# A graph network on one core: the six products of a split adjacency tile in another order, with both waits ahead of them

## The chip, the cores and the metric

The kernel runs on one core of one Trainium2 chip. The metric is the device time in microseconds (us) of one execution. The kernel before took 1182.28 us, the median of 3 runs (1181.62 to 1182.28).

## The reference

Four graph layers run one after the other over the same 4096 x 4096 adjacency matrix `adj` and a 4096 x 128 feature matrix `x`, each followed by a residual sum and a layer norm:

```python
deg = clip(sum(adj, axis=1), 1.0)
x = layernorm(x + x @ L0_W_self + (adj @ x / deg) @ L0_W_neigh)
x = layernorm(x + relu(adj @ (x @ L1_kernel) + L1_bias))
h = relu(adj @ (x @ L2_W1) + b1);  h = relu(adj @ (h @ L2_W2) + b2)
x = layernorm(x + h)
n1 = swish((adj @ x) @ L3_W + b);  n2 = swish((adj @ n1) @ L3_W + b)
x = layernorm(x + n2)
```

So the adjacency matrix is multiplied six times by a 4096 x 128 operand. Everything is float32.

## The kernel before

Six passes (numbered 0 to 5) go over the adjacency matrix, one for each product with it. A pass makes 8 chunks of 512 output columns, and a chunk is summed in one bank of `agg` over 16 tiles of 128 x 1024 (two blocks of 512 columns, which are two steps of the contraction). Of a chunk's tiles 14 come again in each pass from HBM into the 7 slots of `ring`, and two stay in `kept` from pass 0 on.

For speed the float32 product is taken apart. ScalarE casts a tile to the rounded type, `adj_hi` (`hi_tile`, L417). VectorE subtracts it from the tile and leaves the rest in `adj_lo` (`lo_tile`, L538). The operand has such halves too, `op_hi` and `op_lo`. A tile then costs TensorE six products of 128 x 512: for each of its two blocks hi x hi, op_lo x adj_hi and op_hi x adj_lo (`tile_split`, L301). In pass 0 only 4 of 16 tiles of a chunk go this way (tiles 3, 7, 11, 15) and 12 are multiplied whole (`tile_whole`, L297); VectorE sums the degrees there too (L533). In passes 1 to 5 every tile is split. There are 4 places for halves (`SPLITS`), so ScalarE may be three tiles ahead of TensorE.

The order on each engine is written out by hand. Each engine walks through the 16 tiles of a chunk, and between them stand the steps that end the chunk before it, at the tile numbers of tables such as `ROWS_AT`, `STATS_AT` and `SHIFT_AT`. For the norm of passes 1, 3 and 5 the order is: ScalarE reads `agg` (L435, L459), VectorE adds (L554, or L575 and L581), in passes 1 and 3 TensorE turns the rows (L334), VectorE takes statistics (L563, L568), GpSimd takes the inverse root (L636, L638), VectorE makes `shift` (L571), ScalarE applies it (L443). All of it is in the engines' queues, in order, between the tiles' casts, subtractions and products. In pass 3 L334 stands right behind tile 4 on TensorE and L571 right ahead of the subtraction of tile 9 on VectorE; in pass 1 L571 stands ahead of tile 9 too; in pass 5 L346 stands behind tile 3 and L571 ahead of tile 12.

SyncE refills a slot of `ring` when VectorE has subtracted its tile (`vec_tile`). ScalarE casts tile t when TensorE has ended tile t-4 (`tile_used`). TensorE waits for `hi_ready` (the cast) and for `vec_tile` (the subtraction), `first_lo` in pass 0.

Of the kernel before, what the change touches and what calls it, by code (L numbers as in the profile page):

```python
# [5 lines left out]
def bass_gnn_residual_norm_kernel(  # L6
# [43 lines left out]
    D = x_t.shape[0]  # L50
    N = x_t.shape[1]
    CHUNKS, TILES = adj_tiles.shape[0], adj_tiles.shape[1]
    NB = N // P
    CW = N // CHUNKS
    BPT = NB // TILES
# [21 lines left out]
    with ctx:  # L77
        def sb(name, shape, dt=fp32):
            return ctx.enter_context(nc.sbuf_tensor(name, shape, dt))
# [10 lines left out]
        op_hi = sb("op_hi", [P, N], fp32r)  # L90
        op_lo = sb("op_lo", [P, N], fp32r)
        kept = sb("kept", [P, CHUNKS * KEPT, TW])
        ring = sb("ring", [P, SLOTS, TW])
        adj_hi = sb("adj_hi", [P, SPLITS, TW], fp32r)
        adj_lo = sb("adj_lo", [P, SPLITS, TW], fp32r)
# [111 lines left out]
        def bank_of(c):  # L207
            return agg[:, bass.ds((c % 2) * CW, CW)]
# [9 lines left out]
        def nth_hi(p, c, t):  # L218

            if p == 0:  # L220
                return len(SPLIT_FIRST) * c + SPLIT_FIRST.index(t) + 1
            return len(SPLIT_FIRST) * CHUNKS + ((p - 1) * CHUNKS + c) * TILES + t + 1
# [5 lines left out]
        def split_place(p, t):  # L228
            return SPLIT_FIRST.index(t) if p == 0 else t % SPLITS
# [40 lines left out]
        def _(pe):  # L270
# [30 lines left out]
            def tile_split(p, c, t):  # L301
                s = split_place(p, t)
                pe.wait_ge(hi_ready, nth_hi(p, c, t))
                for b in range(BPT):
                    j = t * BPT + b
                    a_hi = adj_hi[:, s, b * CW:(b + 1) * CW]
                    nc.tensor.matmul(bank_of(c), op_hi[:, j * D:(j + 1) * D], a_hi, start=(j == 0), stop=False)  # L307
                    nc.tensor.matmul(bank_of(c), op_lo[:, j * D:(j + 1) * D], a_hi, start=False, stop=False)  # L308
                if p == 0:
                    pe.wait_ge(first_lo, nth_hi(p, c, t))  # L310
                else:
                    pe.wait_ge(vec_tile, (p * CHUNKS + c) * TILES + t + 1)
                for b in range(BPT):
                    j = t * BPT + b
                    last = nc.tensor.matmul(bank_of(c), op_hi[:, j * D:(j + 1) * D],  # L315
                                            adj_lo[:, s, b * CW:(b + 1) * CW], start=False, stop=(j == NB - 1))
                last.then_inc(tile_used, 1)

            def post(p, c, at):
# [30 lines left out]
            def chunk(p, c, posted):  # L350
                first = isinstance(c, int) and c == 0
                final = isinstance(c, int) and c == CHUNKS - 1
                for t in range(TILES):
                    if p == 0:
                        if first and t % (TILES // X_PARTS) == 0:
                            pe.wait_ge(x_loaded[t * X_PARTS // TILES], 16)
                        if t in SPLIT_FIRST:
                            if first:
                                pe.wait_ge(x0_lo, SPLIT_FIRST.index(t) + 1)
                            tile_split(p, c, t)  # L360
                        else:
                            tile_whole(c, t)
                    else:
                        if first and (t == 0 or t >= EARLY[p]):
                            ready = max(EARLY[p], t + 1)
                            pe.wait_ge(gen_lo, (p - 1) * TILES + ready)
                        tile_split(p, c, t)
                    if posted:
                        post(*posted, t)
                    if p in GEN_PASSES and first and EARLY[p] <= t + GEN_LEAD[p] < TILES:  # L370
                        gen(p, t + GEN_LEAD[p])
                    if p + 1 in GEN_PASSES and final and t < EARLY[p + 1]:
                        gen(p + 1, t)
# [297 lines left out]
```

## Time and profile before

| | |
|---|---|
| median of 3 runs | 1182.28 us |
| span of the profiled execution (first to last instruction) | 1180.8 us |
| TensorE products busy | 1161.3 us, 98%, 5056 products and as many loads |
| TensorE weight loads busy (beside the products) | 898.0 us, 76% |
| VectorE busy | 1043.4 us, 88% |
| ScalarE busy | 822.2 us, 70% |
| DMA, mean rate | 312 GB/s |
| TensorE on the chain of waits that ends last | 92% |

For the profiled execution the page gives the span alone; the median of the runs is 1.5 us above it. PE is TensorE's product queue, PEld its weight loads, DVE is VectorE, ACT ScalarE, POOL GpSimd, SP SyncE. A product's duration in the profile holds its way through the array, so that two products in a row overlap in it: what a product costs in a stream is the distance from its start to the next one's. In the timeline a row stands for one or several like instructions (x2), with the start in us, the time from the first's start to the last's end, and in brackets the idle time before it and what ended that.

### The profile page before, as it was taken

The page shows a single profiled execution, that of the slowest core. Times are in us where ns is not written, and L with a number is a line of the kernel's source. Part 1 is how long each engine was busy: PE and PEld are TensorE (multiplying, and loading weights), DVE is VectorE, ACT ScalarE, POOL GpSimd, SP SyncE. Part 2 cuts the span into 40 slices and gives each one's busy share as a digit, 9 for nine tenths or more (in the row PEclk, how much of TensorE's full clock was granted, in tenths as well). Part 3 has the DMA queues.
Part 4 walks back from the last instruction along what each step waited for, and adds up shares of the span by engine and source line. Part 5 has one row for each costly group of instructions (what it writes and reads, how often), then busy time and mean ns, then how long its engine had stood idle before and what let it go on. Part 6 is the DMA issues. An engine that isn't in the chain of part 4 may idle for free.

```text
span 1180.8 us, 18560 instructions
## 1 busy us (share of the span) xinstructions
PE 1161.3 (98%) x5056; PEld 898.0 (76%) x5056; DVE 1043.4 (88%) x1260; ACT 822.2 (70%) x1014; POOL 84.4 (7%) x72
## 2 busy tenths in 40 slices
PE   7999999999999999999999999999999999999996
PEld 3555555678888888888888888877888888888885
DVE  6999999988898889888888989999988899899896
ACT  1232222368878878778777888898877888878884
POOL 0000100001011000000000010010000000001101
PEclk9999999999999999999999999999999999999998
DMA  9988888788889978999987999998999988899992
GB/s 347 343 271 307 290 301 290 270 294 297 326 312 333 329 243 305 363 339 331 347 301 269 343 323 328 330 325 295 353 334 346 328 312 314 290 323 341 329 329 111
DMA packets 106945, 367.92 MB, mean 312 GB/s; under 512 B 11808, under 2 KB 16800, under 8 KB 106912
## 3 DMA queue, kind: packets, MB, share of 16 engines
q1 hardware_dynamic: 100096, 362.85, 85.5%
q10 hardware_dynamic: 6816, 4.66, 1.3%
q8 instruction: 17, 0.28, 0.1%
q14 instruction: 16, 0.13, 0.0%
HBM read 365.36 MB, written 2.10 MB: 311 GB/s over the span
## 4 chain that ended last, share of the span: by engine, by line
PE 92%; DVE 4%; DMA 1%; issue 1%; ACT 1%; POOL 0%; SPq 0%; DVEq 0%; POOLq 0%; ACTq 0%
PE agg L315 25%; PE agg L307 25%; PE agg L308 25%; PE agg L297 12%; PE p_gen L288 2%; DVE adj_lo L538 2%; DMA kept<-adj_tiles 1%; DVE deg_part L533 1%; PE p_mix L328 1%; PE p_turn L339 1%; PE p_mix L346 1%; PE p_rows L329 1%; PE p_rows L334 1%; ACT t_x L443 0%; DVE op_lo L522 0%
## 5 line engine op out<-in xcount | busy, mean ns | idle before, releaser
L538 DVE TENSOR_TENSOR adj_lo<-ring,adj_hi 128x1024 fp32r<-128x1024 f32 x584 | 692.6, 1219 | 40.3 <-ACT adj_hi L417 24.5
L417 ACT CAST adj_hi<-ring 128x1024 fp32r<-128x1024 f32 x584 | 603.3, 1054 | 149.5 <-PE agg L315 97.4
L307 PE MATMUL agg<-adj_hi,op_hi 128*128 128x512 f32 x1344 | 543.0, 404 | 0.8 <-ACT adj_hi L417 0.5
L308 PE MATMUL agg<-adj_hi,op_lo 128*128 128x512 f32 x1344 | 524.4, 390 | 0.0
L315 PE MATMUL agg<-adj_lo,op_hi 128*128 128x512 f32 x1344 | 416.5, 391 | 0.8 <-DVE adj_lo L538 0.8
L307 PEld LDWEIGHTS agg<-adj_hi,op_hi 128*128 128x128 f32 x1344 | 252.6, 188 | 59.3 <-issue 6.6
L315 PEld LDWEIGHTS agg<-adj_lo,op_hi 128*128 128x128 f32 x1344 | 250.7, 188 | 59.2 <-DVE adj_lo L538 6.5
L308 PEld LDWEIGHTS agg<-adj_hi,op_lo 128*128 128x128 f32 x1344 | 252.9, 188 | 54.6 <-issue 6.0
L297 PE MATMUL agg<-ring,hidden 128*128 128x512 f32 x352 | 160.8, 600 | 5.5 <-DMA ring<-adj_tiles 5.5
L533 DVE TENSOR_TENSOR deg_part<-deg_part,ring 128x1024 f32<-128x1024 f32 x104 | 126.8, 1219 | 5.4 <-DMA ring<-adj_tiles 3.3
L297 PEld LDWEIGHTS agg<-ring,hidden 128*128 128x128 f32 x352 | 65.7, 193 | 71.6 <-issue 69.8
L538 DVE TENSOR_TENSOR adj_lo<-kept,adj_hi 128x1024 fp32r<-128x1024 f32 x88 | 105.9, 1222 | 15.8 <-ACT adj_hi L417 13.8
L636 POOL TENSOR_SCALAR var_eps<-moments 128x4 f32<-128x4 f32 x32 | 34.5, 1079 | 1088.4 <-DVE moments L568 1088.4
L417 ACT CAST adj_hi<-kept 128x1024 fp32r (+1 forms) x88 | 91.3, 1055 | 13.9 <-PE agg L315 11.8
L638 POOL TENSOR_TENSOR rstd<-var_eps,minus_half 128x4 f32<-128x4 f32 x32 | 49.1, 1535 | 2.7
L443 ACT ACTIVATE t_x<-t_y,shift,rstd 128x128 f32<-128x128 f32 x64 | 26.4, 483 | 30.4 <-DVE shift L571 30.4
L408 ACT CAST op_hi<-p_gen 128x256 fp32r<-128x256 f32 x48 | 17.9, 373 | 33.0 <-PE p_gen L288 33.0
L430 ACT ACTIVATE t_act<-p_mix,rdeg 128x128 f32<-128x128 f32 x32 | 9.1, 369 | 31.6 <-DVE rdeg L546 31.6
L571 DVE SCALAR_TENSOR_TENSOR shift<-moments,rstd 128x4 f32<-128x4 f32 x32 | 5.1, 161 | 25.8 <-POOL rstd L638 25.8
L522 DVE TENSOR_TENSOR op_lo<-p_gen,op_hi 128x256 fp32r<-128x256 f32 x48 | 19.9, 418 | 7.0 <-ACT op_hi L408 6.9
L426 ACT COPY t_in<-agg 128x512 f32 (+1 forms) x8 | 4.7, 586 | 29.2 <-PE agg L315 29.2
L533 DVE TENSOR_TENSOR deg_part<-deg_part,kept 128x1024 f32<-128x1024 f32 x16 | 19.5, 1222 | 5.7 <-DMA kept<-adj_tiles 5.2
(60 smaller groups left out, 418.5 us busy)
## 6 DMA issues: line engine op xcount, KB each, us to landing
ring<-adj_tiles SPq DMA_DIRECT2D x672, 512.0 KB, 5.3
kept<-adj_tiles SPq DMA_DIRECT2D x8, 1024.0 KB, 7.9
hidden<-x_blocks SPq DMA_DIRECT2D x8, 256.0 KB, 9.8
xT<-x_t ACTq DMA_DIRECT2D x8, 256.0 KB, 2.9
out<-t_x ACTq DMA_DIRECT2D x8, 256.0 KB, 6.1
w<-W ACTq DMA_DIRECT2D x2, 64.0 KB, 9.0
w_self<-W_self ACTq DMA_DIRECT2D x1, 64.0 KB, 6.2
w_neigh<-W_neigh ACTq DMA_DIRECT2D x1, 64.0 KB, 6.9
```

The costliest lines, as they stand in the source:

```text
L288: last = nc.tensor.matmul(dst, src[:, j * P:(j + 1) * P], w[:], start=True, stop=True)
L297: last = nc.tensor.matmul(bank_of(c), hidden[:, j * D:(j + 1) * D], raw[:, b * CW:(b + 1) * CW], start=(j == 0), stop=(j == NB - 1))
L307: nc.tensor.matmul(bank_of(c), op_hi[:, j * D:(j + 1) * D], a_hi, start=(j == 0), stop=False)
L308: nc.tensor.matmul(bank_of(c), op_lo[:, j * D:(j + 1) * D], a_hi, start=False, stop=False)
L315: last = nc.tensor.matmul(bank_of(c), op_hi[:, j * D:(j + 1) * D], adj_lo[:, s, b * CW:(b + 1) * CW], start=False, stop=(j == NB - 1))
L417: nc.scalar.copy(adj_hi[:, split_place(p, t), :], raw_tile(c, t)).then_inc(hi_ready, 1)
L443: nc.scalar.activation(dst, rows[:, b * D:(b + 1) * D], ACT.Identity, bias=shift[:, b:b + 1], scale=rstd[:, b:b + 1]).then_inc(norm_ready, 1)
L522: nc.vector.tensor_tensor(op_tile(op_lo, t), value, op_tile(op_hi, t).bitcast(fp32), ALU.subtract).then_inc(gen_lo, 1)
L533: nc.vector.tensor_tensor(deg_part[:], deg_part[:], raw_tile(c, t), ALU.add).then_inc(vec_tile, 1)
L538: nc.vector.tensor_tensor(adj_lo[:, s, :], raw_tile(c, t), adj_hi[:, s, :].bitcast(fp32), ALU.subtract).then_inc(vec_tile if p else first_ ...
L636: nc.gpsimd.tensor_scalar(var_eps[:], moments[:, :, 1], EPS, None, ALU.add).then_inc(var_ready, 1)
L638: nc.gpsimd.tensor_tensor(rstd[:], var_eps[:], minus_half[:], ALU.pow).then_inc(rstd_ready, 1)
```

## The change

The six products of a split tile get another order: for each block hi x hi, then op_hi x adj_lo, then op_lo x adj_hi, so that the two products with the weights `op_hi` of a block follow each other. Since `adj_lo` is now read by the second product, the wait for it stands beside the wait for `adj_hi`, ahead of all six; before it stood behind the fourth.

```diff
             def tile_split(p, c, t):
                 s = split_place(p, t)
                 pe.wait_ge(hi_ready, nth_hi(p, c, t))
-                for b in range(BPT):
-                    j = t * BPT + b
-                    a_hi = adj_hi[:, s, b * CW:(b + 1) * CW]
-                    nc.tensor.matmul(bank_of(c), op_hi[:, j * D:(j + 1) * D], a_hi, start=(j == 0), stop=False)
-                    nc.tensor.matmul(bank_of(c), op_lo[:, j * D:(j + 1) * D], a_hi, start=False, stop=False)
                 if p == 0:
                     pe.wait_ge(first_lo, nth_hi(p, c, t))
                 else:
                     pe.wait_ge(vec_tile, (p * CHUNKS + c) * TILES + t + 1)
                 for b in range(BPT):
                     j = t * BPT + b
-                    last = nc.tensor.matmul(bank_of(c), op_hi[:, j * D:(j + 1) * D],
-                                            adj_lo[:, s, b * CW:(b + 1) * CW], start=False, stop=(j == NB - 1))
+                    blk = slice(b * CW, (b + 1) * CW)
+                    w_hi = op_hi[:, j * D:(j + 1) * D]
+                    nc.tensor.matmul(bank_of(c), w_hi, adj_hi[:, s, blk], start=(j == 0), stop=False)
+                    nc.tensor.matmul(bank_of(c), w_hi, adj_lo[:, s, blk], start=False, stop=False)
+                    last = nc.tensor.matmul(bank_of(c), op_lo[:, j * D:(j + 1) * D], adj_hi[:, s, blk],
+                                            start=False, stop=(j == NB - 1))
                 last.then_inc(tile_used, 1)
```

The order on TensorE, in the loop over the chunks of pass 3, from the turn of the rows (L334, behind tile 4) through tile 5. `agg<-adj_hi,op_lo` is a product with the moving operand `adj_hi` and the weights `op_lo`; in brackets stand the semaphores it waits for. Before:

```order
L334 MATMUL p_rows<-ident,t_y 128x128 [waits y_ready]
L334 MATMUL p_rows<-ident,t_y 128x128 x3
L307 MATMUL agg<-adj_hi,op_hi 128x512 [waits hi_ready]
L308 MATMUL agg<-adj_hi,op_lo 128x512
L307 MATMUL agg<-adj_hi,op_hi 128x512
L308 MATMUL agg<-adj_hi,op_lo 128x512
L315 MATMUL agg<-adj_lo,op_hi 128x512 [waits vec_tile]
L315 MATMUL agg<-adj_lo,op_hi 128x512
```

And now, at the same place:

```order
L333 MATMUL p_rows<-ident,t_y 128x128 [waits y_ready]
L333 MATMUL p_rows<-ident,t_y 128x128 x3
L312 MATMUL agg<-adj_hi,op_hi 128x512 [waits vec_tile,hi_ready]
L313 MATMUL agg<-adj_lo,op_hi 128x512
L314 MATMUL agg<-adj_hi,op_lo 128x512
L312 MATMUL agg<-adj_hi,op_hi 128x512
L313 MATMUL agg<-adj_lo,op_hi 128x512
L314 MATMUL agg<-adj_hi,op_lo 128x512
```

The wait for `vec_tile` has gone from the fifth product to the first, four products forward, and the first and second product of each block have the same weights.

In pass 0 the same, on TensorE, from the whole tile ahead of a split one (here tiles 2 and 3 of a chunk in the loop; `first_lo` counts the subtractions of pass 0). Before:

```order
L297 MATMUL agg<-ring,hidden 128x512 [waits slot_loaded2]
L297 MATMUL agg<-ring,hidden 128x512
L303 ISA
L307 MATMUL agg<-adj_hi,op_hi 128x512 [waits hi_ready]
L308 MATMUL agg<-adj_hi,op_lo 128x512
L307 MATMUL agg<-adj_hi,op_hi 128x512
L308 MATMUL agg<-adj_hi,op_lo 128x512
L315 MATMUL agg<-adj_lo,op_hi 128x512 [waits first_lo]
```

And now:

```order
L297 MATMUL agg<-ring,hidden 128x512 [waits slot_loaded2]
L297 MATMUL agg<-ring,hidden 128x512
L303 ISA
L312 MATMUL agg<-adj_hi,op_hi 128x512 [waits first_lo,hi_ready]
L313 MATMUL agg<-adj_lo,op_hi 128x512
L314 MATMUL agg<-adj_hi,op_lo 128x512
```

Here too the wait for the subtraction stands four products earlier. The number of products and weight loads is the same, and nothing moves on the other engines.

## Rows read from the trace of the kernel before

**Rows 1.** Windows: stretch, length, busy PE, PEld, DVE, ACT, POOL, PEclk, DMA, GB/s.

```profile
500.00:600.00 100.00, 100.00 (x447) 82.98 (x446) 88.29 (x75) 79.21 (x81) 0.00 (x0) 1.00 0.92 338
```

**Rows 2.** The page's groups by line: busy us, mean ns | idle before.

```profile
L538 DVE TENSOR_TENSOR adj_lo<-ring,adj_hi 128x1024 fp32r<-128x1024 f32 x584 | 692.6, 1219 | 40.3 <-ACT adj_hi L417 24.5
...
L307 PE MATMUL agg<-adj_hi,op_hi 128*128 128x512 f32 x1344 | 543.0, 404 | 0.8 <-ACT adj_hi L417 0.5
...
L307 PEld LDWEIGHTS agg<-adj_hi,op_hi 128*128 128x128 f32 x1344 | 252.6, 188 | 59.3 <-issue 6.6
```

**Rows 3.** Timeline of TensorE in pass 2: start us, us, instruction.

```profile
565.68 0.39 PE L307 MATMUL agg<-adj_hi,op_hi 128*128 128x512 f32 x1
...
567.04 0.39 PE L307 MATMUL agg<-adj_hi,op_hi 128*128 128x512 f32 x1
```

**Rows 4.** Waits: who waited for whom, us in total, times, longest.

```profile
DVE shift L571 <- POOL rstd L638: 25.8, 24, 1.6
...
DVE t_y L575 <- PE p_mix L346: 7.8, 8, 3.0
...
DVE t_y L554 <- ACT t_in L435: 7.4, 7, 1.4
...
PEld agg L315 <- DVE adj_lo L538: 6.5, 19, 1.0
```

**Rows 5.** Waits of VectorE, pass 3 alone.

```profile
DVE stats L563 <- PE p_rows L334: 1.0, 5, 0.2
```

**Rows 6.** Timeline of the end of pass 3: chunk 7, tile 9.

```profile
793.33 1.22 DVE L538 TENSOR_TENSOR adj_lo<-ring,adj_hi 128x1024 fp32r<-128x1024 f32 x1
...
792.96 0.39 PE L307 MATMUL agg<-adj_hi,op_hi 128*128 128x512 f32 x1
...
794.60 0.74 PE L315 MATMUL agg<-adj_lo,op_hi 128*128 128x512 f32 x2 [0.58 <-DVE adj_lo L538]
795.18 0.40 PE L307 MATMUL agg<-adj_hi,op_hi 128*128 128x512 f32 x1
```

**Rows 7.** Timeline of pass 3, chunk 3, tile 9.

```profile
703.12 0.17 DVE L571 SCALAR_TENSOR_TENSOR shift<-moments,rstd 128x4 f32<-128x4 f32 x1 [1.24 <-POOL rstd L638]
703.22 3.50 DVE L538 TENSOR_TENSOR adj_lo<-ring,adj_hi 128x1024 fp32r<-128x1024 f32 x3
...
703.76 0.39 PE L307 MATMUL agg<-adj_hi,op_hi 128*128 128x512 f32 x1
```

**Rows 8.** Timeline of pass 5, chunk 4, tile 14.

```profile
1097.61 2.36 DVE L538 TENSOR_TENSOR adj_lo<-kept,adj_hi 128x1024 fp32r<-128x1024 f32 x2 [0.57 <-ACT adj_hi L417]
...
1097.98 0.39 PE L307 MATMUL agg<-adj_hi,op_hi 128*128 128x512 f32 x1
```

**Rows 9.** Timeline of pass 5, chunk 7, tile 14 (the last such one).

```profile
1166.01 2.36 DVE L538 TENSOR_TENSOR adj_lo<-kept,adj_hi 128x1024 fp32r<-128x1024 f32 x2 [0.39 <-ACT adj_hi L417]
...
1166.58 0.39 PE L307 MATMUL agg<-adj_hi,op_hi 128*128 128x512 f32 x1
```

**Rows 10.** Timeline of pass 1, tile 9 of chunk 3 and of chunk 6.

```profile
333.34 2.36 DVE L538 TENSOR_TENSOR adj_lo<-ring,adj_hi 128x1024 fp32r<-128x1024 f32 x2
...
333.84 0.39 PE L307 MATMUL agg<-adj_hi,op_hi 128*128 128x512 f32 x1
...
401.27 2.36 DVE L538 TENSOR_TENSOR adj_lo<-ring,adj_hi 128x1024 fp32r<-128x1024 f32 x2
...
402.09 0.39 PE L307 MATMUL agg<-adj_hi,op_hi 128*128 128x512 f32 x1
```

**Rows 11.** Timeline of pass 0, chunk 0: the last split tile and what precedes it.

```profile
33.71 1.95 PE L297 MATMUL agg<-kept,hidden 128*128 128x512 f32 x4 [1.08 <-DMA kept<-adj_tiles]
...
35.07 1.22 DVE L538 TENSOR_TENSOR adj_lo<-kept,adj_hi 128x1024 fp32r<-128x1024 f32 x1
35.21 0.68 PE L307 MATMUL agg<-adj_hi,op_hi 128*128 128x512 f32 x1
```

**Rows 12.** Line L307: sequencer's work, min/median/max ns.

```profile
L307 PEldq FUSED_REGOPS  x30: 99/99/99, 274.4 to 1123.3; - x30
```

## The prediction

> **What bounds the kernel now.** I read the windows first. From 500 to 600 us TensorE's products fill the whole window at granted clock 1.00, its upper level of 2.4 GHz; VectorE works 88 of the 100 us, ScalarE 79, and the DMA engines stand at 0.92 [rows 1]. A busy PE could still be a slow PE, so the timeline comes next: the first product of one tile starts at 565.68, that of the next at 567.04 [rows 3]. That is 1.36 us for six products, 0.227 us each, with no hole between them. The groups agree: over 1344 products of L307 the engine stood idle 0.8 us in all [rows 2]. So in passes 1 to 5 whatever TensorE loses is lost for good, unless it is waiting at the end of that stretch anyway.
>
> The second question is how far ahead VectorE is, since the wait for its low half is what moves. A subtraction takes 1.22 us [rows 2], and in a row they start about 1.14 us apart (three in 3.50 us, [rows 7]: (3.50 - 1.22) / 2). That is 0.22 us per tile faster than TensorE, so mostly VectorE is ahead. It falls back once in every chunk that ends with a norm: it stands in its queue until GpSimd has the inverse root, 24 times, 25.8 us in all [rows 4], and the subtractions of the next tiles stand behind that wait. There I looked at when the low half of a tile is ready and when TensorE starts the tile. VectorE takes the tiles in TensorE's order, so the tiles are found by the code: L571 stands right ahead of the subtraction of tile 9 (12 in pass 5).
>
> **What the change does, part by part.**
>
> Count of work: six products and six weight loads per tile before and after, the same DMAs, nothing moved on VectorE, ScalarE, GpSimd or SyncE. The cost of the products themselves I take as unchanged, 0.227 us each: a load of 0.188 us lies under the product ahead of it [rows 2]. (The first rival takes this up.)
>
> The wait for `vec_tile` or `first_lo` moves from the fifth product to the first, which is 4 x 0.227 = 0.91 us earlier. It can only cost. At the old place TensorE's loads stood for it 19 times, 6.5 us in all [rows 4]; those waits stay, and each becomes up to 0.91 us longer. New ones come wherever the low half is ready less than a margin before the first product.
>
> The margin is read from a place where TensorE does wait: the low half is ready at 793.33 + 1.22 = 794.55, two products (L315) follow, and the next tile starts at 795.18 [rows 6]. From ready to there are 0.63 us, where two products in a stream take 0.45. So a tile behind a wait goes as if it had started 0.18 us after its low half was ready. The bounds are 0 (the load goes ahead and only the product waits) and 0.40 (ready to the second product's start: 0.63 less one spacing, with nothing of it overlapped). I take 0.18, because it is measured at this very wait.
>
> The price of a place is then: low half ready + 0.18 - start of the tile.
> - Pass 3, tile 9: ready at 703.22 + 1.22 = 704.44, the tile starts at 703.76 [rows 7]. 0.68 + 0.18 = 0.86 us. Chunks 1 to 6 look alike, within 0.02 us: 6 x 0.86 = 5.2 us.
> - Pass 3, last chunk: the low half is ready at 794.55, the tile starts at 792.96, and TensorE already waits inside the tile [rows 6]. There the price is the four products, 0.91 us, and for the tiles behind it nothing, since there VectorE sets the pace and all move together.
> - Pass 5, tile 14: ready at 1097.61 + 1.22 = 1098.83, the tile starts at 1097.98 [rows 8]. 0.85 + 0.18 = 1.03 us, the worst of its chunk (tile 12 lacks less). Six chunks: 6.2 us. The seventh: 1167.23 against 1166.58 [rows 9], 0.65 + 0.18 = 0.83. Together 7.0 us. The eighth norm comes when no tile is left.
> - Pass 1, tile 9: 0.72 + 0.18 = 0.90 us in chunk 3 (334.56 against 333.84), 0.40 + 0.18 = 0.58 in chunk 6 (402.49 against 402.09) [rows 10], depending on how long GpSimd takes. Six chunks, and one of the same kind in the first chunk of pass 2: 7 x 0.70 (about the middle) = 4.9 us.
> - Pass 4, first chunk, the norm that ends pass 3: TensorE waits inside the tile, as in [rows 6], but the chain is partly the one already paid for at the end of pass 3. Between 0 and 0.91; I take 0.3.
> - Pass 0: in the first chunk each of the 4 split tiles starts just as its subtraction does. Three delays are taken in by the 1.08 us in which TensorE stands for the `kept` transfer at 33.71; the last (ready at 36.29, start at 35.21) is not [rows 11]: 0.91 us. In the later chunks VectorE is further ahead: 0.
>
> Do these add up? Within a chunk no: one delay serves all tiles behind it, since VectorE, being late, is not made later by it; I have counted only the worst tile. From chunk to chunk yes: the chain that makes VectorE late begins each time at TensorE itself. VectorE stood for L346's products 8 times in pass 5, for the read of the ended chunk (L554 behind L435) 7 times [rows 4], and in pass 3 for the turned rows 5 times [rows 5]. So each chunk starts its race anew from TensorE's delayed time, and the delay is paid again.
>
> Two waits in front of one product: in the built order some tiles get a register instruction that waits for `hi_ready`. Register work of the PE sequencer lasts 99 ns a piece [rows 12]. I cost it at nothing: the cast is always ready at least one subtraction (1.22 us) before the low half, so this wait is long over when the other ends, and the sequencer runs under products of 0.227 us. With that cover gone it would be up to 0.1 us x 672 tiles = 67 us (the third rival).
>
> Sum: 5.2 + 0.9 + 7.0 + 4.9 + 0.3 + 0.9 = 19.2 us. On the profiled span, 1180.8 + 19.2 = 1200.0. The median of the runs lies 1.5 us above the span, so 1201.5; with small lags at chunk starts that I haven't counted, 1202 us, 1.7% slower.
>
> The sum's own ends: margin 0 instead of 0.18 at the 20 places that use it (6 + 7 + 7) takes off 3.6, pass 4 at 0 another 0.3, so +15.3. Margin 0.40 adds 4.4, pass 4 at 0.91 adds 0.6, and the two earlier delays of pass 0 that the `kept` wait may not hold add 1.8: +26. That is 1198 to 1208.5.
>
> **The rivals.**
>
> 1. Products with the weights already in place are cheaper. In 1344 of 4032 products (2 of 6 in each tile) the weights are those of the product before. For it: 0.227 us a product is 545 cycles of 2.4 GHz for 512 columns; if the rest over one cycle a column (213 ns, an estimate from the row's shape and clock) were the change of weights, 14 ns go at 1344 products: -18.8 us, and the result is 1202 - 19 = 1183, no slower than before. Against it: every product of L307 has its own load in the trace, x1344 of 188 ns [rows 2], shorter than the 227 ns of the product that hides it; the count of products in the built order is unchanged and each carries its weights. The trace of before has no two products in a row with the same weights, so it can't decide. The Trainium skill ("TensorE: Matmul & The Clock Gate", Part 2: What happens when you issue a matmul) gives the load as a separate step because weights usually stay for many matmuls: load once, multiply repeatedly. No run here shows a repeat without a load; were the repeats' spacing the page's isolated figure of about 216 ns, an estimate from that page is (227 - 216) x 1344 = 15 us back, and the result 1187.
>
> 2. The waits cost nothing: VectorE's or ScalarE's chain moves so that the lags are absorbed once and not per chunk. For it: VectorE gains 0.22 us per tile, 3.6 us per chunk. Against it: it has gained them all in the rows above and is still late at those tiles. Only one delay per pass would stay, about 5 x 0.9 = 4.5: 1187.
>
> 3. The double wait is not hidden: each tile pays 0.05 to 0.1 us at the start, 34 to 67 us: 1236 to 1269. For it only the instruction in the built order; against it the register work that already stands ahead of each tile in the loops and leaves no hole [rows 3].
>
> 4. The change doesn't move the wait in the machine, because the product's wait is held with its load. The built order shows it in front of the first product, so this is all but excluded; it would give 1182.
>
> **How the numbers follow.** Forecast 0.80; rival 1 0.07 (split about evenly between within 0.2% and faster, since the spacing could fall by up to the 39 ns between the load's 188 and 227, which would be 52 us, 1150); rival 2 0.06; rival 3 0.05; rival 4 0.02. A change of under 0.2%, 2.4 us, can't be told from none. Slower: 0.80 + 0.06 + 0.05 = 0.91; within 0.2%: 0.02 + 0.03 = 0.05; faster: 0.04. The forecast's own range is 1198 to 1208.5; the range to hold 8 in 10 is let out on both sides for places I took as alike without pricing each, 1194 to 1211.
>
> **What would show it.** Right: the first product of a split tile (the new L312) gets waits for `adj_lo` L538, some 20 long ones, of about 0.5 to 1.1 us each; the other two lines get none; spacing stays 0.227; loads stay 5056; pass 2 and pass 4 grow by under 2 us, pass 3 by about 6, pass 5 by about 7, pass 1 by about 4.5. VectorE's idle time grows by as much. Wrong: a spacing other than 0.227 for the second product of a block (rival 1), a hole ahead of every tile (rival 3), or passes 1, 3 and 5 growing by under 1.5 us each (rival 2).

## The result, and the profile after

The changed kernel takes 1200.3 us (median of 4 runs, 1199.88 to 1200.76) against 1182.03 for the kernel before (4 runs, one more than in the table above, 1181.62 to 1182.28): ratio 1.0155, 95% interval 1.0140 to 1.0169. It is slower by 18.3 us; the forecast was 1202 us, 20 more, with a range of 1198 to 1208.5. The profiled execution's span is 1198.5 us, 17.7 more than before.

First the page's groups by line of the kernel after (busy us, mean ns | idle before, and what ended it):

```profile
L537 DVE TENSOR_TENSOR adj_lo<-ring,adj_hi 128x1024 fp32r<-128x1024 f32 x584 | 695.0, 1219 | 46.5 <-ACT adj_hi L416 27.8
...
L312 PE MATMUL agg<-adj_hi,op_hi 128*128 128x512 f32 x1344 | 547.6, 407 | 11.3 <-DVE adj_lo L537 9.6
L314 PE MATMUL agg<-adj_hi,op_lo 128*128 128x512 f32 x1344 | 524.7, 390 | 0.0
L313 PE MATMUL agg<-adj_lo,op_hi 128*128 128x512 f32 x1344 | 523.9, 390 | 0.0
L312 PEld LDWEIGHTS agg<-adj_hi,op_hi 128*128 128x128 f32 x1344 | 252.5, 188 | 88.1 <-DVE adj_lo L537 19.4
L314 PEld LDWEIGHTS agg<-adj_hi,op_lo 128*128 128x128 f32 x1344 | 252.3, 188 | 54.5
L313 PEld LDWEIGHTS agg<-adj_lo,op_hi 128*128 128x128 f32 x1344 | 252.8, 188 | 53.0 <-issue 6.0
```

The durations are those of before [rows 2]. What is new is idle time ahead of L312, the first product of a block, and so of a tile, ended by the subtraction; the other two lines have none. L313 has the weights of L312 and still its own 1344 loads of 188 ns. The waits of the kernel after say the same (of the loads' 35 waits for the subtraction 24 last 0.49 to 1.01 us, where some 20 of 0.5 to 1.1 were forecast), and the three that tie VectorE's chain to TensorE are all there again as in [rows 4, 5]:

```profile
PEld agg L312 <- DVE adj_lo L537: 19.4, 35, 1.0
...
DVE t_y L574 <- PE p_mix L345: 11.9, 8, 3.9
...
DVE t_y L553 <- ACT t_in L434: 8.3, 7, 1.4
...
DVE stats L562 <- PE p_rows L333: 1.7, 7, 0.3
```

The place of [rows 7], pass 3, chunk 3, tile 9, in the timeline after (start, us; in brackets the idle time and what ended it):

```profile
709.95 0.17 DVE L570 SCALAR_TENSOR_TENSOR shift<-moments,rstd 128x4 f32<-128x4 f32 x1 [1.24 <-POOL rstd L637]
710.04 2.36 DVE L537 TENSOR_TENSOR adj_lo<-ring,adj_hi 128x1024 fp32r<-128x1024 f32 x2
...
711.32 0.50 PE L312 MATMUL agg<-adj_hi,op_hi 128*128 128x512 f32 x1 [0.58 <-DVE adj_lo L537]
711.66 0.40 PE L313 MATMUL agg<-adj_lo,op_hi 128*128 128x512 f32 x1
...
712.82 0.39 PE L312 MATMUL agg<-adj_hi,op_hi 128*128 128x512 f32 x1
```

The low half is ready at 710.04 + 1.22 = 711.26, and the next tile starts at 712.82, 1.56 us later, where six products in a stream take 1.36. That is 0.20 us of margin, where 0.18 was taken. One chunk later the first product of tile 9 starts at 726.04 before and at 734.46 after:

```profile
726.04 0.39 PE L307 MATMUL agg<-adj_hi,op_hi 128*128 128x512 f32 x1
```

```profile
734.46 0.51 PE L312 MATMUL agg<-adj_hi,op_hi 128*128 128x512 f32 x1 [0.59 <-DVE adj_lo L537]
```

The tile of chunk 3 was 7.56 us behind the one of before (711.32 against 703.76), this one is 8.42 behind: 0.86 us more. The same at the place of [rows 8], pass 5, chunk 4, tile 14:

```profile
1111.65 1.23 DVE L537 TENSOR_TENSOR adj_lo<-kept,adj_hi 128x1024 fp32r<-128x1024 f32 x1 [0.56 <-ACT adj_hi L416]
...
1112.93 0.50 PE L312 MATMUL agg<-adj_hi,op_hi 128*128 128x512 f32 x1
...
1114.43 0.40 PE L312 MATMUL agg<-adj_hi,op_hi 128*128 128x512 f32 x1
```

Here the margin is 0.19 us (1114.43 - 1112.88 - 1.36).

Where the time went by pass is read from the first split product of each pass. After:

```profile
248.96 0.40 PE L312 MATMUL agg<-adj_hi,op_hi 128*128 128x512 f32 x1
444.85 0.47 PE L312 MATMUL agg<-adj_hi,op_hi 128*128 128x512 f32 x1
628.37 0.47 PE L312 MATMUL agg<-adj_hi,op_hi 128*128 128x512 f32 x1
815.85 0.47 PE L312 MATMUL agg<-adj_hi,op_hi 128*128 128x512 f32 x1 [0.52 <-ACT adj_hi L416]
997.08 0.39 PE L312 MATMUL agg<-adj_hi,op_hi 128*128 128x512 f32 x1
```

And before:

```profile
249.32 0.40 PE L307 MATMUL agg<-adj_hi,op_hi 128*128 128x512 f32 x1
441.37 0.39 PE L307 MATMUL agg<-adj_hi,op_hi 128*128 128x512 f32 x1
623.80 0.39 PE L307 MATMUL agg<-adj_hi,op_hi 128*128 128x512 f32 x1
804.43 0.51 PE L307 MATMUL agg<-adj_hi,op_hi 128*128 128x512 f32 x1 [0.28 <-DVE op_lo L522]
985.69 0.39 PE L307 MATMUL agg<-adj_hi,op_hi 128*128 128x512 f32 x1
```

| pass | before, us | after, us | more | forecast |
|---|---|---|---|---|
| 0 (to the first row) | 249.3 | 249.0 | -0.4 | +0.9 |
| 1 | 192.0 | 195.9 | +3.8 | +4.2 |
| 2 | 182.4 | 183.5 | +1.1 | +0.7 |
| 3 | 180.6 | 187.5 | +6.9 | +6.1 |
| 4 | 181.3 | 181.2 | 0.0 | +0.3 |
| 5 (to the span's end) | 195.1 | 201.4 | +6.3 | +7.0 |

### The profile page after: what moved, and what is told of

It is laid out like the page before. It is cut to its first block, busy times and chain, and to the rows that moved or that the text cites. A ratio compares the mean times of both kernels' runs of the same rounds, so it can differ in the third digit from the quotient of the medians.

```text
span 1198.5 us, 18729 instructions
## 1 busy us (share of the span) xinstructions
PE 1171.1 (98%) x5056; PEld 895.4 (75%) x5056; DVE 1047.6 (87%) x1260; ACT 826.9 (69%) x1014; POOL 83.6 (7%) x72
## 4 chain that ended last, share of the span: by engine, by line
PE 76%; DVE 9%; issue 5%; POOL 5%; ACT 2%; DMA 2%; SPq 0%; DVEq 0%; POOLq 0%; ACTq 0%
PE agg L312 20%; PE agg L314 20%; PE agg L313 19%; PE agg L297 11%; DVE adj_lo L537 5%; POOL rstd L637 3%; PE p_gen L288 2%; POOL var_eps L635 2%; ACT adj_hi L416 1%; DVE stats L562 1%; DMA kept<-adj_tiles 1%; DVE deg_part L532 1%; PE p_mix L327 1%; DMA ring<-adj_tiles 1%; DVE moments L567 1%
## 5 line engine op out<-in xcount | busy, mean ns | idle before, releaser
L312 PE MATMUL agg<-adj_hi,op_hi 128*128 128x512 f32 x1344 | 547.6, 407 | 11.3 <-DVE adj_lo L537 9.6
L313 PE MATMUL agg<-adj_lo,op_hi 128*128 128x512 f32 x1344 | 523.9, 390 | 0.0
L312 PEld LDWEIGHTS agg<-adj_hi,op_hi 128*128 128x128 f32 x1344 | 252.5, 188 | 88.1 <-DVE adj_lo L537 19.4
L313 PEld LDWEIGHTS agg<-adj_lo,op_hi 128*128 128x128 f32 x1344 | 252.8, 188 | 53.0 <-issue 6.0
L416 ACT CAST adj_hi<-kept 128x1024 fp32r (+1 forms) x88 | 91.8, 1051 | 19.3 <-PE agg L314 16.8
```

Of the source, the lines that this page charges most:

```text
L312: nc.tensor.matmul(bank_of(c), w_hi, adj_hi[:, s, blk], start=(j == 0), stop=False)
L313: nc.tensor.matmul(bank_of(c), w_hi, adj_lo[:, s, blk], start=False, stop=False)
L416: nc.scalar.copy(adj_hi[:, split_place(p, t), :], raw_tile(c, t)).then_inc(hi_ready, 1)
```

## The experiments

The theory: TensorE loses at about 20 places of an execution where VectorE is late with the low half, each by how much too early the wait stands. Rivals: the order of the products or pairs of equal weights are worth something; two waits on one product cost; the lag is VectorE's whole work and not its wait for GpSimd. Times of the kernel before beside the runs: 1182.18 us (15 runs) for the first four, 1182.37 (21) for the next four, 1182.28 (21) for the last three.

**The wait alone, and the order alone.** The old order with both waits first:

```diff
                 pe.wait_ge(hi_ready, nth_hi(p, c, t))
+                (the wait for first_lo or vec_tile)
                 for b in range(BPT):
                     ... hi x hi, lo weights x hi
-                (the wait for first_lo or vec_tile)
                 for b in range(BPT):
                     ... hi weights x adj_lo
```

> The products in the old order (hi x hi, lo weights, for each block, then the two with adj_lo), but both waits ahead of the first. Theory (the early wait for the subtraction is the whole of the loss): 1200.3 us as the changed kernel, within 1.5 us, with pass 3 again about 7 us and pass 5 about 6 us longer than before. Rival (the order of the products, with equal weights in a row, costs or gives something): a time that differs from 1200.3 by what the order is worth, higher if pairs of equal weights give time back, lower if they cost some.

Measured: 1200.34 us, ratio 1.0154 (1.0139 to 1.0170). The whole loss is there without any change of the products' order, and by pass it lies where it lay (3.8, 1.1, 6.8, 0.0 and 6.3 us in passes 1 to 5). This kernel has none of the 1344 pairs of equal weights and the changed kernel has all; their times, 1200.34 and 1200.30, do not differ beyond the noise, so the pairs are worth nothing. TensorE's loads stood for the subtraction 35 times, 19.3 us, against 35 times, 19.4 us, in the changed kernel.

The counterpart has one pair of equal weights in each tile and the wait where it was:

```diff
-                    matmul(op_hi[j], a_hi);  matmul(op_lo[j], a_hi)     # for b = 0, 1
+                    matmul(op_lo[j], a_hi);  matmul(op_hi[j], a_hi)
                 (the wait for first_lo or vec_tile)
-                for b in range(BPT):
+                for b in reversed(range(BPT)):
                     matmul(op_hi[j], adj_lo)
```

> The wait stays behind the fourth product as before; the products are ordered so that the fourth and the fifth have the same weights (op_hi of the second block). One pair of equal weights per tile, 672 in all, no earlier wait. Theory (a repeat of the weights is worth nothing, it is loaded again under the product ahead): 1182.0 us, within 0.2%, and 0.227 us from the fourth product to the fifth. Rival (the repeat is cheaper, by 14 to 39 ns): 1156 to 1173 us.

Measured: 1182.29 us, ratio 0.9999 (0.9990 to 1.0008). In its timeline in pass 2, L308 at 566.18 has the weights of the first of the two L315 at 566.41:

```profile
566.18 0.39 PE L308 MATMUL agg<-adj_hi,op_hi 128*128 128x512 f32 x1
566.41 0.61 PE L315 MATMUL agg<-adj_lo,op_hi 128*128 128x512 f32 x2
```

The distance is 0.23 us as everywhere. A pair of equal weights is worth nothing in this kernel. Each product still has its own load (1344 on each of the three lines), 188 ns long under the 227 ns of the product ahead. What a repeat without a load would cost, no run shows.

**One wait instead of two.**

```diff
                 s = split_place(p, t)
-                pe.wait_ge(hi_ready, nth_hi(p, c, t))
```

> The changed kernel without the wait for hi_ready at the split tiles (the subtraction waits for the cast itself, so the wait for the subtraction stands for both). Theory (the second wait is hidden): 1200.3 us, within 1.5 us. Rival (two waits on one product hold up the sequencer): several us less, up to the whole difference of 18 us.

Measured: 1200.36 us, ratio 1.0154 (1.0139 to 1.0170). The second wait is hidden, as costed.

**The wait moved product by product.** Three kernels put it behind the first, second and third product; the order is only changed as far as the data needs it. The first of them:

```diff
                 for b in range(BPT):
                     ...
                     matmul(w_hi, adj_hi)
+                    if b == 0: (the wait for first_lo or vec_tile)
                     matmul(w_hi, adj_lo)
```

> The new order, but the wait for the subtraction stands behind the first product, where its data is first needed. Theory: each of about 20 late tiles gets 0.227 us back, one product, so 1200.3 - 4.5 = 1195.8 us, still slower than before by 1.1 to 1.2%. Rival (not the lateness but the doubling of waits ahead of one product, or the new order, costs the time): with one wait per product again as before, 1182 to 1185 us if it is the doubling, 1200 if it is the order.

The other two go by a list of weights, tile half and block; the wait stands ahead of number 2 of the first and number 3 of the second:

```diff
-                (products and wait as before)
+                products = [('hi', 'hi', 0), ('lo', 'hi', 0), ('hi', 'lo', 0), ('hi', 'hi', 1), ('lo', 'hi', 1), ('hi', 'lo', 1)]
+                products = [('hi', 'hi', 0), ('lo', 'hi', 0), ('hi', 'hi', 1), ('hi', 'lo', 0), ('lo', 'hi', 1), ('hi', 'lo', 1)]
```

> The wait for the subtraction behind the second product (block 0: hi x hi, lo weights, then the one with adj_lo; block 1 the same), no two equal weights in a row. Theory (each product that the wait stands later gives 0.227 us back at each place that is still late): 7 x 0.45 in pass 5, 6 x 0.42 in pass 3 and one at its end of 0.45, 7 x 0.11 in pass 1: 1182 + 7 = 1189 us. Rival (the first product's wait is dear for a reason of its own, the later ones are nearly free): 1182 to 1184 us.

> The wait for the subtraction behind the third product. Theory: 7 x 0.22 in pass 5, 6 x 0.19 in pass 3 and 0.2 at its end, none in pass 1: 1182 + 3 = 1185 us. Rival as for the wait behind the second: 1182 us.

| the wait stands behind | us | over the kernel before beside it | ratio, 95% |
|---|---|---|---|
| 0 products (changed kernel) | 1200.30 | 18.3 | 1.0140 to 1.0169 |
| 1 | 1193.75 | 11.6 | 1.0083 to 1.0114 |
| 2 | 1188.95 | 6.6 | 1.0043 to 1.0073 |
| 3 | 1184.68 | 2.3 | 1.0012 to 1.0031 |
| 4 (kernel before) | 1182.2 | 0 | |

The steps are 6.7, 5.0, 4.3 and 2.3 us. Divided by 0.227 us they stand for 29, 22, 19 and 10 places: fewer are late with every step. The second and third rung came out as forecast (1189 and 1185); the first missed by 2 us, 1193.75 for 1195.8. Each place did give back about what was forecast (pass 3, tile 9, slips 0.63 us a chunk there where it slipped 0.87). Left out were small lags, which went altogether: at the start of five chunks (0.27 to 0.35 us each, in passes 1 to 3) and at tile 6 of five chunks of pass 1 (0.1 each), some 2 us together. No step stands out, so the first wait isn't dear for a reason of its own.

**VectorE's wait for GpSimd.** The changed kernel with the step that waits for GpSimd one tile later:

```diff
-        SHIFT_AT = {0: 12, 1: 9, 3: 9, 5: 12}
-        NORM_AT = {0: 14, 1: 11, 3: 12, 5: 14}
+        SHIFT_AT = {0: 12, 1: 10, 3: 10, 5: 13}
+        NORM_AT = {0: 14, 1: 11, 3: 12, 5: 15}
```

> The changed kernel with VectorE's wait for GpSimd (the step that makes shift) one tile later in passes 1, 3 and 5, and ScalarE's norm of pass 5 one tile later (SHIFT_AT 9, 9, 12 to 10, 10, 13; NORM_AT of pass 5 14 to 15). Theory (the price is that this wait stands ahead of the subtractions): in pass 3 the lag of 0.86 us goes in six chunks, in pass 5 that of 0.91 shrinks to that of tile 8, 0.24, in seven, in pass 1 0.58 shrinks to 0.1 in six: 1200.3 - 5.3 - 4.7 - 2.8 = 1187.5 us. Rival (VectorE's whole work per chunk sets the lag, wherever the wait stands): within 2 us of 1200.3.

Measured: 1193.41 us, ratio 1.0097 (1.0081 to 1.0112). Seven us came back, not 13. By pass, read from the first products as above: pass 1 took 193.0 us (195.9 in the changed kernel, 2.9 less, 2.8 forecast), pass 3 183.4 (187.5; 4.1 less, 5.3 forecast), but pass 5 202.5 (201.4, 1.1 more where 4.7 less was forecast). The timeline of pass 5, chunk 4, shows what the later norm ran into:

```profile
1101.53 1.65 ACT L442 ACTIVATE t_x<-t_y,shift,rstd 128x128 f32<-128x128 f32 x4
1103.36 0.38 ACTq L465 DMA_DIRECT2D out<-t_x  x1
1103.96 1.05 ACT L416 CAST adj_hi<-kept 128x1024 fp32r x1 [0.78 <-ACT t_x L442]
...
1105.15 1.23 DVE L537 TENSOR_TENSOR adj_lo<-kept,adj_hi 128x1024 fp32r<-128x1024 f32 x1 [2.04 <-ACT adj_hi L416]
...
1106.44 0.50 PE L312 MATMUL agg<-adj_hi,op_hi 128*128 128x512 f32 x1 [0.56 <-DVE adj_lo L537]
```

With the norm at tile 15 it stands right ahead of the output's store, which waits for it (`STORE_AT`, 15). ScalarE's cast of tile 15 is held for norm and store, VectorE stands 2.04 us for that cast, and TensorE for VectorE. The lag of tile 14 had become one of tile 15. The miss in pass 3 is GpSimd's: the inverse root took 1.86 us instead of 1.04 (below), so tile 10 is late now, and about 0.35 us per chunk stayed in six chunks, where nothing was to stay. That is 2.1 us; 1.0 us came back at the last chunk, which the forecast did not count.

The same edit in the old order:

> The kernel before with the same two steps one tile later. Theory: only the few places gain where TensorE stood for the subtraction in the old order too (about 2 us at the end of pass 3 and in the first chunk of pass 4, 0.1 us in each of six chunks of pass 5): 1179.5 us. Rival (TensorE's stream holds nothing more to win by it, or later norms make new waits): 1182 to 1184 us.

Measured: 1180.69 us, ratio 0.9986 (0.9977 to 0.9995): a little faster than before, by 1.7 us; 1179.5 was forecast. Pass 3 gave 1.2 us and pass 5 0.4; pass 4 took 0.3 more.

**GpSimd's own chain.** VectorE adds eps, in place of GpSimd's first step:

```diff
                     for b in range(BPC):
                         nc.vector.bn_aggr(moments[:, b, :], stats[:, b, :]).then_inc(moments_ready, 1)
+                    dve.wait_ge(moments_ready, BPC * (nth(NORM_PASSES, p, c) + 1))
+                    dve.nop(nofuse=True)
+                    nc.vector.tensor_scalar(var_eps[:], moments[:, :, 1], EPS, None, ALU.add).then_inc(var_ready, 1)
...
-                pool.wait_ge(moments_ready, BPC * (n + 1))
-                pool.nop(nofuse=True)
-                nc.gpsimd.tensor_scalar(var_eps[:], moments[:, :, 1], EPS, None, ALU.add).then_inc(var_ready, 1)
                 pool.wait_ge(var_ready, n + 1)
+                pool.nop(nofuse=True)
```

> The changed kernel with the same step moved to VectorE. Theory (GpSimd's chain makes VectorE late, and part of that chain is GpSimd standing behind VectorE's own subtraction): the lag falls by about 0.3 us in six chunks of pass 3, 0.5 in six of pass 1, and from 0.91 to 0.3 in seven of pass 5: 1200.3 - 1.8 - 3.0 - 4.3 = 1191 us. Rival (the lag is VectorE's own work, not its wait for GpSimd): 1200.3 or up to 5 us more, since VectorE gets 0.2 us more to do per norm.

Measured: 1194.68 us, ratio 1.0106 (1.0091 to 1.0122), 5.6 us less than the changed kernel where 9 were forecast. Pass 5 lost 2.6 us against before (6.3 without the edit), pass 1 1.8 (3.8), pass 3 6.7 (6.9). VectorE has more to do than before, and the time fell: the lag is its wait, not its work. The forecast failed in pass 3 for the reason told under the hardware below: with GpSimd's first step gone, its second starts beside a subtraction and takes 1.9 us instead of 1.04.

The same edit in the old order:

> The kernel before, with the first of GpSimd's two steps per norm (variance + eps on 128 x 4 numbers) done by VectorE right behind the moments. That GpSimd step took 1.03 us beside a subtraction and 0.23 us where VectorE was idle; the inverse root took 1.04 us with VectorE idle and 1.86 beside a subtraction. Theory: shift is ready about 1.1 us earlier in passes 1 and 5 and 0.3 us in pass 3, and the few places where TensorE still stood for the subtraction get shorter: 1180 us. Rival (nothing left to win in the old order): 1182 us, or more by VectorE's own 32 x 0.2 us if its time counts.

Measured: 1181.13 us, ratio 0.9990 (0.9981 to 0.9999) where 1180 was forecast. The gain is in pass 5 (1.1 us).

The last one has the old order, eps on VectorE as above, and

```diff
-        SHIFT_AT = {0: 12, 1: 9, 3: 9, 5: 12}
+        SHIFT_AT = {0: 12, 1: 10, 3: 10, 5: 12}
```

> The kernel before with eps on VectorE and with shift one tile later in passes 1 and 3 (pass 5 left as it was). Theory: the gains of both add up where TensorE stood for the subtraction, at the end of pass 3, the start of pass 4 and in pass 5: 1179.5 us, the fastest of all. Rival: no better than the one with later steps alone, 1180.7 us.

Measured: 1180.25 us, ratio 0.9982 (0.9973 to 0.9991); 1179.5 was forecast. It beats both kernels, by 2 us and by 20. Against the one with the later steps alone (1180.69) the difference is too small to tell. In it TensorE's loads still stand for the subtraction 12 times:

```profile
PEld agg L315 <- DVE adj_lo L538: 3.6, 12, 0.4
```

## Why the prediction was right, and where it was off

The main step held: nothing is gained by the order, the wait alone costs, and the cost per place is ready time plus margin minus the tile's start. The wait alone gave the whole loss, the order alone none, and the ladder shows the price per product.

That the delays add from chunk to chunk held too. In pass 3 tile 9 slips by a further 0.82 to 0.89 us in every chunk, 0.87 in the mean (0.86 forecast), and VectorE's three waits for TensorE's side are in the profile after.

Rival 1 (equal weights are cheaper) fell with the kernel that has the pair and the old wait, and with the one that has the early wait and no pair; rival 2 (absorbed once per pass) with the even slips; rival 3 (double wait) with the kernel without the second wait; rival 4 with the first.

The total is nearer than its terms, which were off in both directions:

- Pass 0, +0.9 forecast, -0.4 measured. The step that failed is "the last is not" taken in: it isn't by the `kept` transfer, but a later wait does it. Of the delay 0.62 us are there behind the first chunk (the next chunk's first split tile starts at 44.98 us, at 44.36 before), and it goes at the end of the next one, where TensorE stands for the norm before it turns the rows. Before and after, in this order:

```profile
60.49 0.33 PE L339 MATMUL p_turn<-ident,t_x 128*128 128x128 f32 x1 [1.09 <-ACT t_x L443]
```

```profile
60.14 0.66 PE L338 MATMUL p_turn<-ident,t_x 128*128 128x128 f32 x4
```

  Before, TensorE had stood 1.09 us for ScalarE there; after, it comes later and hardly waits. At that place none of VectorE's steps stands for TensorE, so its chain and ScalarE's norm behind it did not move with TensorE. That takes the delay to 0. The sign is chance: in the profiled execution after, both engines ran 0.34 us earlier than before, from the first `kept` transfer at the latest (VectorE starts on it at 33.26 us, before at 33.60), and over all the kernels here pass 0 ends between 248.2 and 249.6 us.
- Pass 5, 7.0 forecast, 6.3 measured: a chunk lost 0.9 us, not 1.03. The end of the lag at tile 14 is right to 0.02 us. The step that failed is that this place was priced as a new wait. TensorE already stood there before the change: the low half was ready at 1098.83, and the products at the old place of the wait were held a little. Before, at [rows 8]:

```profile
1098.89 0.74 PE L315 MATMUL agg<-adj_lo,op_hi 128*128 128x512 f32 x2
1099.46 0.39 PE L307 MATMUL agg<-adj_hi,op_hi 128*128 128x512 f32 x1
```

  From the first L315 to the next tile there are 0.57 us where two products in a stream take 0.45, so 0.12 us of the margin was paid already, in each of chunks 1 to 6. The prediction's own words on such places ("each becomes up to 0.91 us longer") give the price: a wait moved by four products costs 4 x 0.227 = 0.91 us where TensorE stood at its old place (the seven chunks lost 0.90 in the mean). The delay also comes in pieces: in chunk 4 at tiles 8, 12 and 14 and the tiles behind the first two, 0.9 us together. That the sum is set by the worst tile held.
- Pass 1, 4.2 forecast, 3.8 measured: the mean of the places was taken from two kinds of chunk, 0.90 and 0.58 [rows 10]. The dear kind came from GpSimd, whose first step took 2.17 us in chunks 3 and 4 of the run before:

```profile
329.91 2.17 POOL L636 TENSOR_SCALAR var_eps<-moments 128x4 f32<-128x4 f32 x1 [19.77 <-DVE moments L568]
```

  In the run after it took 1.03 in every chunk. Chunks 2 to 6 lost 0.57 to 0.59 us each and chunk 1 0.74, of which 0.27 lie at its first two tiles. The dear kind is no property of the chunk: in the kernel without the second wait GpSimd's step took 2.17 us in chunk 3 alone of this pass, and that chunk lost 0.91 us, as priced.
- Passes 2 and 3 lost 0.4 and 0.8 more than forecast. At the first two chunks of each the first tile slips by 0.17 to 0.23 us and the second by another 0.11 to 0.12; these were named as small lags and not priced beyond 0.5 us, and come to 1.3 together. Against that, the place in the first chunk of pass 2 cost 0.4 us, not 0.7. And 0.24 us of pass 3's row lie at the first tile of pass 4, whose second tile makes them good.

So the errors partly cancel: 19.2 forecast, 17.7 in the span. One sign missed: VectorE's idle time was to grow by as much as the time, and grew by 13.5 us (137.4 to 150.9). The Trainium skill's reason for a separate load, weights that stay for many products ("TensorE: Matmul & The Clock Gate", Part 2), was not at work here: 1344 repeats each kept a load of their own.

## What to carry to other kernels

A wait in front of a run of products costs by how late its data is at the few worst places, not by how late it is on average: VectorE was ahead of TensorE nearly everywhere, and the change cost 18 us at some 25 places. Put the products that need the late operand last, and put each wait as late as the data allows. Where the engine stood for the same data before the change, the price is the products that the wait moved over. Whether such delays add is read from the waits that tie the late engine back to TensorE; where there is one in each chunk, each chunk pays again.

## What the runs showed of the hardware

GpSimd's two steps on 128 x 4 numbers took longer beside a subtraction of VectorE. (The profile's durations on GpSimd are rough.) In the kernel before, the first step of the last norm, with VectorE idle, and the one that follows:

```profile
1174.96 0.23 POOL L636 TENSOR_SCALAR var_eps<-moments 128x4 f32<-128x4 f32 x1 [11.81 <-DVE moments L568]
1175.27 1.04 POOL L638 TENSOR_TENSOR rstd<-var_eps,minus_half 128x4 f32<-128x4 f32 x1
```

Beside a subtraction the first takes 1.03 us and the second 1.86, here in the kernel after, pass 5, chunk 4:

```profile
1105.38 2.32 DVE L537 TENSOR_TENSOR adj_lo<-ring,adj_hi 128x1024 fp32r<-128x1024 f32 x2
...
1105.62 1.03 POOL L635 TENSOR_SCALAR var_eps<-moments 128x4 f32<-128x4 f32 x1 [20.79 <-DVE moments L567]
1106.74 1.86 POOL L637 TENSOR_TENSOR rstd<-var_eps,minus_half 128x4 f32<-128x4 f32 x1
```

With eps on VectorE (changed order), pass 5:

```profile
1101.23 2.36 DVE L537 TENSOR_TENSOR adj_lo<-ring,adj_hi 128x1024 fp32r<-128x1024 f32 x2
...
1101.43 1.90 POOL L638 TENSOR_TENSOR rstd<-var_eps,minus_half 128x4 f32<-128x4 f32 x1 [21.33 <-DVE var_eps L570]
...
1103.51 0.15 DVE L573 SCALAR_TENSOR_TENSOR shift<-moments,rstd 128x4 f32<-128x4 f32 x1
```

The subtraction had begun 0.20 us ahead and ends at 1102.45; the inverse root ends at 1103.33, 0.88 us later. VectorE's second subtraction meanwhile runs at its usual 1.22 us. The Trainium skill ("SBUF — State Buffer", SBUF: two separate sides) has VectorE's operations with two SBUF inputs and GpSimd's operations that read SBUF share a port pair as an exclusive lock, for the whole instruction, on which the loser blocks. The trace agrees for GpSimd: its inverse root ends 0.88 us behind the subtraction, 0.86 us later than its 1.04 us alone would have it, as if it had stood until the subtraction was over. It does not agree for VectorE, which isn't held by the rest of the inverse root. So a short GpSimd step between two VectorE steps should be started while VectorE does something else. This was not tried by itself.
